# A state-space layer between two feed-forward layers: the causal convolution and the residual adds move from TensorE to VectorE, and B and C share one product

## The reference

```python
x = x + 0.5 * ffn(layernorm(x))           # w = int4-simulated kernel; y = x @ w + bias + (x @ a) @ b
x = x + mamba(layernorm(x))               # this one adds its own input again
x = x + 0.5 * ffn(layernorm(x))

def mamba(x):                             # h = layernorm(x) * norm_w + norm_b
    x_ssm, z = split(h @ Win)
    x_ssm = silu(depthwise_conv(x_ssm, conv_w, 4 taps, causal) + conv_b)
    dt = softplus(x_ssm @ dt_w + dt_b)
    A, B, C = -exp(A_log), x_ssm @ Bp, x_ssm @ Cp
    state[t] = state[t-1] * exp(dt[t] * A) + (dt[t] * x_ssm[t]) * B[t]
    y[t] = sum over states of state[t] * C[t]
    y = (y + x_ssm * D) * silu(z)
    return x + y @ Wout
```

## Time and profile before

| what | value |
|---|---|
| median of 3 runs | 5839.85 us (5838.22 to 5840.39) |
| the profiled execution | 5846.96 us, its span 5845.0 us |
| granted TensorE clock, mean over the span | 0.974 |
| block starts (first scan), blocks 1 to 14 | 543.6 to 5154.2 us, some 354.7 us apart |
| HBM read, written | 875.74 MB, 88.08 MB |
| DMA engines, mean busy share | about 0.5 |

### The profile page before, as it was taken

One profiled execution on the slowest core, in us unless ns is written; L12 is line 12 of the kernel. 1 busy time (PEld: TensorE's weight loads), 2 busy tenths in 40 slices (PEclk: granted clock), 3 DMA queues, 4 the chain that ended last, 5 costly groups with the idle time before them and its releaser, 6 DMA issues.

```text
span 5845.0 us, 206313 instructions
## 1 busy us (share of the span) xinstructions
PE 5374.8 (92%) x86664; PEld 3347.2 (57%) x86664; DVE 4834.3 (83%) x4323; ACT 4067.0 (70%) x6785; POOL 5097.9 (87%) x2326
## 2 busy tenths in 40 slices
PE   5798999989899998999989999898999989999887
PEld 2455656556565555655656565565655656565554
DVE  0689888888888888888888888888888888898996
ACT  3767676776767677676776777767676776866664
POOL 0689898998989889898898988989899898999996
PEclk9899999999999999999999999999999999999999
DMA  5465554656546565555656556555465655656553
GB/s 153 156 156 193 137 185 171 158 186 148 189 152 172 180 151 185 148 171 179 158 191 140 180 171 155 194 145 187 152 176 183 151 186 146 175 180 159 198 176 115
DMA packets 578961, 977.34 MB, mean 167 GB/s; under 512 B 294881, under 2 KB 328450, under 8 KB 510466
## 3 DMA queue, kind: packets, MB, share of 16 engines
q1 hardware_dynamic: 313858, 961.82, 53.1%
q10 hardware_dynamic: 264192, 2.11, 2.8%
HBM read 875.74 MB, written 88.08 MB: 165 GB/s over the span
## 4 chain that ended last, share of the span: by engine, by line
PE 41%; POOL 33%; issue 18%; DVE 3%; ACT 3%; DMA 2%; POOLq 0%; DVEq 0%; ACTq 0%; SPq 0%
POOL H L605 30%; PE pUB L690 14%; PE Y L716 13%; PE pP L645 4%; DVE H L570 3%; PE pP L638 2%; DMA Cb<-scratch_c 2%; PE pP L663 2%; PE pA L742 2%; PE pP L651 1%; POOL lnv L619 1%; ACT dA L434 1%; POOL dto L623 1%; PE pA L735 1%; PE pA L729 1%
## 5 line engine op out<-in xcount | busy, mean ns | idle before, releaser
L570 DVE TENSOR_TENSOR_SCAN H<-dA,pUB 128x512 f32<-128x512 f32 x4096 | 4697.0, 1203 | 791.4 <-PE pUB L690 733.0
L605 POOL TENSOR_TENSOR H<-H,Cb 128x1024 f32<-128x1024 f32 x2048 | 4811.1, 2390 | 512.6 <-DVE H L570 492.6
L434 ACT ACTIVATE dA<-DT,w_negA 128x512 f32<-128x512 f32 x4096 | 2615.4, 710 | 1130.3 <-DVE H L570 1126.4
L690 PEld LDWEIGHTS pUB<-Bd,UT 64*64 64x64 f32 x65536 | 1952.5, 135 | 1291.9 <-issue 1278.9
L690 PE MATMUL pUB<-Bd,UT 64*64 64x128 f32 x65536 | 2274.9, 275 | 298.7 <-DVE H L570 227.6
L716 PE MATMUL Y<-H,w_ident 64*64 64x512 f32 x16384 | 2018.9, 603 | 63.0 <-POOL H L605 60.7
L716 PEld LDWEIGHTS Y<-H,w_ident 64*64 64x64 f32 x16384 | 659.2, 136 | 650.1 <-issue 641.9
L434 ACT ACT_TABLE_LOAD x224 | 287.4, 1283 | 4.0
L638 PE MATMUL pP<-hT,w_Win 128*128 128x512 f32 x512 | 263.7, 639 | 16.0 <-ACT uto L422 12.7
L645 PE MATMUL pP<-xs,w_taps 128*128 128x512 f32 x512 | 252.9, 617 | 4.2 <-ACT xs L373 2.9
L651 PE MATMUL pP<-U,w_dt_w 128*128 128x512 f32 x512 | 252.7, 617 | 3.4 <-ACT zo L386 3.4
(11 more groups left out here) (85 smaller groups left out, 2308.0 us busy)
## 6 DMA issues: line engine op xcount, KB each, us to landing
Cb<-scratch_c SPq DMA_DIRECT2D x512, 1024.0 KB, 5.2
Bd<-scratch_diag SPq DMA_DIRECT2D x512, 512.0 KB, 4.0
scratch_diag<-H SPq DMA_DIRECT2D x16, 1024.0 KB, 17.8
scratch_z<-zo SPq DMA_DIRECT2D x64, 256.0 KB, 5.7
scratch_dt<-dto SPq DMA_DIRECT2D x64, 256.0 KB, 5.8
scratch_ut<-uto SPq DMA_DIRECT2D x64, 256.0 KB, 6.3
DT<-scratch_dt SPq DMA_DIRECT2D x64, 256.0 KB, 5.1
UT<-scratch_ut SPq DMA_DIRECT2D x64, 256.0 KB, 5.5
```

What stands on the lines that cost most here:

```text
L434: last = nc.scalar.activation(dA[:, n % DAR, j, :], DT[:, k, :], ACT.Exp, scale=c["negA"][:, k, GS * blk + j:GS * blk + j + 1])
L570: last = nc.vector.tensor_tensor_scan(H[:, n % HR, 2 * i + j, :], dA[:, n % DAR, 2 * i + j, :], pUB[:, i, :].rearrange("p (t s) -> p s t", ...
L605: nc.gpsimd.tensor_tensor(h[:, j:j + 2, :], h[:, j:j + 2, :], Cb[:, blk % 2, j:j + 2, :], ALU.mult).then_inc(times_c, 1)
L690: last = nc.tensor.matmul(out, UT[rows, k, j * P + h * HP:j * P + h * HP + HP], Bd[rows, blk % 2, i, j * P:(j + 1) * P].rearrange("p (t s) ...
```

## The change

- The four taps are applied by DVE. `convolve(s, m, i)` reads the projection in PSUM, with the tap as a per-partition scalar: the first pass (i = 0) is a multiplication of all 512 columns, the other three multiply and add onto `cv` in SBUF, each shifted by one more column. One pass follows each of the four scans of units 2, 6, 10 and 14. The copy to `xs` and the diagonal matrices go. ACT's silu reads `cv`.
- The residual adds are made by DVE while it reads `pA` (`add_back`), after the second scan of units 11 and 15 (X2), 27 and 32 (X1), 42 and 46 (output). The products with the identity and ACT's copies go. The bias is one product of 512 columns for two parts.
- B and C are one product with 128 output rows in two parts. ACT copies it to `BC`, four PE transposes turn the 64 rows of B, and ACT copies those to `BT`. C is stored from `BC`.
- The table changes with it: x projections at 0, 4, 8, 12; silu at 5, 9, 13, 17; B and C at 20, the transposes at 23, the copy of B at 26, its stores at 27 to 35.

```diff
-ACTS = {"xs": (2, 4, 12, 14), "u": (7, 10, 17, 20), "B": (23,), "store B": (24, 25, 26, 27, 28, 30, 31, 32), "C": (26,), "dt": (29, 34, 41, 48), "log": (30, 35, 42, 49),
-        "z": (31, 38, 45, 52), "turn u": (36, 43, 50, 56), "keep u": (57, 59), "x2": (11, 15),
+ACTS = {"u": (5, 9, 13, 17), "BC": (23,), "B": (26,), "store B": (27, 28, 30, 31, 32, 33, 34, 35), "dt": (29, 34, 41, 48),
+        "log": (30, 35, 42, 49), "z": (31, 38, 45, 52), "turn u": (36, 43, 50, 56), "keep u": (57, 59),
...
-        "turn 1": (18, 21), "x1": (27, 32), "turn c": (35, 37), "out": (42, 46), "turn 3": (58, 60)}
-DVES = {"norm 1": (4,), "norm c": (21,), "norm 2": (40,), "norm 3": (52,), "soft": (30, 35, 42, 49)}
+        "turn 1": (18, 21), "turn c": (35, 37), "turn 3": (58, 60)}
+DVES = {"norm 1": (4,), "norm c": (21,), "norm 2": (40,), "norm 3": (52,), "soft": (30, 35, 42, 49),
+        "conv": (2, 6, 10, 14), "x2": (11, 15), "x1": (27, 32), "out": (42, 46)}
...
-PES = {"xs": (0, 2, 10, 12), "conv": (4, 7, 14, 17), "B": (20,), "C": (23,), "dt": (26, 31, 38, 45), "z": (29, 36, 43, 50),
+PES = {"xs": (0, 4, 8, 12), "BC": (20,), "turn b": (23,), "dt": (26, 31, 38, 45), "z": (29, 36, 43, 50),
...
-                nc.scalar.activation(U[:, m, :], pP[:, :], ACT.Silu, bias=c["conv_b"][:, m:m + 1]).then_inc(u_done, 1)
+                nc.scalar.activation(U[:, m, :], cv[:, :], ACT.Silu, bias=c["conv_b"][:, m:m + 1]).then_inc(u_done, 1)
...
+            def convolve(s, m, i):
+
+                j = DC - 1 - i
+                if i == 0:
+                    dve.wait_ge(mm_x, at(s + 1))
+                    dve.wait_ge(u_done, at(s))
+                    nc.vector.tensor_scalar(cv[:, :], pP[:, :], c["conv_w"][:, m, j:j + 1], None, ALU.mult).then_inc(tap, 1)
+                    return
+                dve.wait_ge(tap, at((DC - 1) * s + i))
+                nc.vector.scalar_tensor_tensor(out=cv[:, i:], in0=pP[:, 0:T - i], scalar=c["conv_w"][:, m, j:j + 1], in1=cv[:, i:],
+                                               op0=ALU.mult, op1=ALU.add).then_inc(tap if j else conv, 1)
+
+            def add_back(out, x, i, done):
+                nc.vector.tensor_tensor(out[:, 2 * i:2 * i + 2, :], pA[:, :, :], x[:, 2 * i:2 * i + 2, :], ALU.add).then_inc(done, 1)
...
-            def turn_b(part):
-
-                for j in (2 * part, 2 * part + 1):
-                    for k in range(KI):
-                        last = nc.tensor.matmul(pP[:, j * DS:(j + 1) * DS], columns(U[:, k, :], j), c["bc_w"][:, k, 0:DS],
-                                                start=(k == 0), stop=(k == KI - 1))
-                if part:
-                    last.then_inc(mm_b, 1)
+            def turn_b():
+
+                for j in range(NJ):
+                    last = nc.tensor.matmul(pP[:, j * DS:(j + 1) * DS], columns(BC[0:DS, :], j), c["ident"][0:DS, 0:DS], is_transpose=True,
+                                            start=True, stop=True)
+                last.then_inc(mm_b, 1)
...
-                nc.tensor.matmul(pA[:, j, :], c["ones"][:, :], c["bias"][:, :], start=True, stop=False)
+                if j == 0:
+                    nc.tensor.matmul(pA[:, :, :].rearrange("p j d -> p (j d)"), c["ones"][:, :], c["bias"][:, :], start=True, stop=False)
...
-                last = keep(j, x, i)
...
-                last = keep(j, X2, i)
```

More of the change, by code:

```diff
@@ L163, in _ @@
             dve.wait_ge(k_small, 11 * 16)
-            link(nc.vector.tensor_scalar(c["bias"][:, :], biasr[:, :], 0.5, None, ALU.mult))
+            for half in range(2):
+                nc.vector.tensor_scalar(c["bias"][:, half * DM:(half + 1) * DM], biasr[:, :], 0.5, None, ALU.mult).then_inc(k_d, 1)
             link(nc.vector.tensor_copy(c["ones"][:, :], one[:, :]))
@@ L168, in _ @@
             dve.wait_ge(k_id, 2)
-            for k in range(KI):
-                for j in range(DC):
-                    nc.vector.tensor_scalar(c["taps"][:, k, j, :], c["ident"][:, :], c["conv_w"][:, k, j:j + 1], None, ALU.mult).then_inc(k_d, 1)
             for k in range(KI):
@@ L467, in step @@
                         silu_z(q, when["z"].index(n))
-                    if close and n in when["out"]:
-                        i = when["out"].index(n)
-                        act.wait_ge(ffnc, at(2 * c_ + i + 1))
-                        nc.scalar.activation(X2[:, 2 * i:2 * i + 2, :], pA[:, :, :], ACT.Copy).then_inc(o_done, 1)
                     if ffn and n == when["norm 1"][0]:
@@ L482, in step @@
                         normalize(nc, act, flip1, X, XN, norm1[3], norm1[4], n1, a)
+                    if proj and n in when["BC"]:
+                        act.wait_ge(mm_bc, at(q + 1))
+                        act.wait_ge(mm_b, at(q))
+                        act.wait_ge(c_st, at(16 * q))
+                        nc.scalar.activation(BC[:, :], pP[:, :], ACT.Copy).then_inc(bc_out, 1)
                     if proj and n in when["B"]:
@@ L488, in step @@
                         store_diagonals(q, when["store B"].index(n))
-                    if proj and n in when["C"]:
-                        act.wait_ge(mm_c, at(q + 1))
-                        act.wait_ge(c_st, at(16 * q))
-                        nc.scalar.activation(Co[:, :], pP[0:DS, :], ACT.Copy).then_inc(c_out, 1)
                     if proj and n in when["dt"]:
@@ L572, in step @@
                                                                     ALU.mult, ALU.add)
-                            last.then_inc(state_done, 1)
+                                if j:
+                                    last.then_inc(state_done, 1)
+                                between(b, n, 2 * i + j, close, proj, ffn)
+                    else:
+                        for i in range(4):
+                            between(b, n, i, close, proj, ffn)
                     if close and n in when["norm c"]:
@@ L855, in macaron @@
         c = {n: sb("w_" + n, s) for n, s in (
[L856 removed]
+            ("ident", [P, P]), ("diagD", [P, KI, P]), ("negA", [P, KI, DS]), ("Wf", [P, KM, DM]), ("bias", [1, 2 * DM]), ("ones", [1, P]),
             ("conv_w", [P, KI, DC]), ("conv_b", [P, KI]), ("dt_b", [P, KI]), ("D", [P, KI]), ("norm_w", [P, KM]), ("norm_b", [P, KM]),
```

99 lines of the change are left out of this document (44 added, 55 removed).

## The result

The changed kernel takes **5660.4 us** (median of 4 runs, 5656.38 to 5668.32) against 5840.1 us for the kernel before (4 runs beside it, 5838.22 to 5843.62): ratio 0.9693, 95% interval 0.9676 to 0.971. That is 180 us or 3.1% less. The forecast was 5680 with a range of 5595 to 5790, so its case came in, 20 us faster than its number. The profiled execution took 5668.32 us, its span is 5666.1 us.

The account below looks back on a forecast made before the run. TensorE sets a unit's pace with more than about 1 us of other work, else VectorE and GpSimd. Gains of 12.9 us a block, 196 in all, less 36 for the clock, gave 5687, as median 5680 us, range 5595 to 5790.

Parts of the forecast that it names:

- Units 21 and 22: B and C in one product makes two parts of 1.92 us, two units of 5.54; gain 6.6 us a block.
- Units 23 to 29: The C product and identity products go, four transposes come, one bias serves two parts; 39.3 to 35.9 us, gain 3.4.
- Units 2 to 20: Convolution moves from TensorE to VectorE, whose passes lengthen four units; 101.7 to 100.0 us, gain 1.7 a block.
- the nearest row is the gate: Convolution pass on VectorE priced like the gate, PSUM times SBUF, at 0.59 us; bounds 0.55 and 0.67.
- of which the unit's slack takes a third: Clock falls behind the convolution: 1.7 us of lost work, partly absorbed, so two falls a block at 1.2 us each.
- Units 30 to 48: TensorE saves 3.9 us, but GpSimd has only 3.3 idle; a third of that taken, gain 1.2, bounds 0 and 3.3.
- the eight B stores are issued three units later, at 27 to 35, and are needed at 62: Later issue of the B stores in units 27 to 35, given no cost.
- Units 49 to 1: Neither VectorE, GpSimd nor the order changes there; gain 0.
- The hold of the softplus pass: Rival: softplus's SBUF pass held elsewhere, 5.7 us a block each; one more 5765 us (one or more, 0.15), none 5595 (0.10).
- The convolution was not held: Rival: convolution passes held like the softplus pass, 1.49 us each, kernel slower at 5896 us; chance 0.07.
- The clock did not fall in units 16 to 20 on top: Rival: clock falls behind every convolution and in units 16 to 20 and 24 to 26, 1.7 us each; 5746 us, 0.10.
- TensorE's time was worth something: Rival: TensorE's time worth nothing, as GpSimd or VectorE is behind it everywhere; 5830 to 5845 us, chance 0.03.

Follow-up runs that it names:

- e1: The kernel before with only B and C in one product, its copy and the transposes that turn B; 5692.5 us.
- e6: The changed kernel with the constant 0.25 as the convolution's tap in all four passes, in place of a per-partition number from SBUF; 5667.0 us in one run.
- e9: The changed kernel with the whole chain of B and C, including the B stores, two units earlier; 5721.6 us.
- e12: The changed kernel without softplus's correction term and with the eight B stores spread over units 27 to 47; 5529.1 us.
- e5: The changed kernel without VectorE's pass in softplus's correction, ScalarE's copy writing zeros that GpSimd subtracts; 5640.5 us.

## Why the prediction was right

It said 12.9 us a block, less 2.4 for the clock, 10.5 in all; the measured gain is 12.1. Its two largest steps were right in mechanism and size; in units 2 to 20 errors of opposite sign cancelled, which is luck. By its own steps:

**Units 21 and 22**, its largest term: 6.6 forecast, 6.7 measured, also alone in e1 (6.6). The 64-column products and the half clock behind them were what made them long: 32 forcing records behind a product now take 1.10 us.

**Units 23 to 29**: 3.4 forecast, 3.9 measured.

**Units 2 to 20**: a gain of 1.7, less two falls of the clock at 1.2 each, so -0.7; measured 0.0. Two sizes in it were off. The pass was taken at 0.59 us from the gate and takes 0.65; the step that failed is "the nearest row is the gate", for the gate has no number per partition, which e6 shows to cost the 0.06. The upper bound, 0.67, held, and so did the Trainium skill's figure that the forecast gave beside its sum (VectorE: DVE Perf Modes, section on the TRN2 errata, 0.66 us). The measured spacing is 0.65, but e6, at 0.60, says that the skill's number met it by another cost. And the falls: 21 in 13 blocks, 1.6 a block in place of 2, but 13 of them at 1.3 to 1.9 us and 8 at 2.7, which is some 3.3 a block in place of 2.4. The step "of which the unit's slack takes a third" was too kind, as VectorE has no slack in this stretch; at unit 15 a fall costs more than its own upper price of 1.7. Against both stands that TensorE runs further ahead than I took: without its falls the stretch would be at some 98.3 us (101.6 - 3.3), where the forecast had 100.0 with cheaper passes. The lengths of units show it. Units 7 and 12, with a part of the out projection, were to take 5.54 us and take 4.46 and 4.44 on average, units 9 and 13 5.09 and 5.23. TensorE in the tenth block, whose unit 7 begins at 3324.47 us:

```profile
3324.06 1.10 PE L701 MATMUL pUB<-Bd,UT 64*64 64x128 f32 x32 [0.71 <-DVE H L586]
3325.10 1.99 PE L749 MATMUL pA<-w_Wout,YG 128*128 128x256 f32 x8
```

It comes out of unit 6 with nothing left to do but wait for the scans, so the 1.99 us of the projection lie under unit 7's.

**Units 30 to 48**: 1.2 forecast from a third of GpSimd's idle time, 0.4 measured. The step that failed is deeper than its size: "the eight B stores are issued three units later, at 27 to 35, and are needed at 62", priced at nothing. By e9 and e12 the place of these stores sets the length of the units around them. The changed kernel lost little by it (its longest issue is 5.1 us, before it 2.3). e1, with the same places of the stores, has 108.3 us there, but by a stop of TensorE with short issues and no late load; that the stores bring this stop is not shown.

**Units 49 to 1**: 0 forecast, 1.0 measured (0.1, 0.1 and 0.8 at the turn). The turn has stops of TensorE behind the loop's jump, and one of them comes and goes between kernels; the forecast has no step for them.

**The rivals.** The hold of the softplus pass landed at unit 49 again: neither 5765 nor 5595. By e5 the price was wrong as well: the whole pass away is worth 20 us, not 85, for the forecast took the length of units 49 to 52 as if nothing were behind VectorE there. Its remark that GpSimd's 2.73 us is less than a whole instruction misreads the rows:

```profile
3561.49 0.67 DVE L579 SCALAR_TENSOR_TENSOR ev<-ev,absv 128x512 f32<-128x512 f32 x1
```

The pass of the kernel before began 0.16 us ahead of the product and had 0.51 us left, so a product held until the pass ended would be 0.51 longer, and it is 0.40 longer.

The convolution was not held (0.718 to 0.752 us in all 256 passes), as the Trainium skill says of one SBUF input (SBUF — State Buffer, section "SBUF: two separate sides"); a tap in SBUF beside cv doesn't count as a second one. The clock did not fall in units 16 to 20 on top. And TensorE's time was worth something almost only in units 21 to 29: of its 27 us a block (408 / 15), 12.1 came out.

## What to carry to other kernels

Price a move stage by stage, by the engine that ends each unit: 14.5 us of TensorE's work a block, taken from a stretch that VectorE then fills, gave nothing on the mean of 13 blocks, and 11 us from one that TensorE filled gave 10.6. When a change shifts DMA issues, count them as work of the queue that issues them and of all 16 engines: many small pieces in a crowd can stop the issuing engine and slow the loads beside them, and spreading them cost nothing and gave 82 us (on the kernel without the correction term). Compare stretches over many blocks before you credit an edit with a difference of the whole, for in this kernel an unrelated stretch moved by 35 us from one edit to the next.
